# Scores of a key tile issued ahead of its first max multiplication, in a one-core attention layer

## The chip, the cores and the metric

One Trainium2 chip, one of its cores. The time is device microseconds (us) of one execution of the whole program on that core; a kernel's time is the median of several executions.

## What is computed

A self-attention layer with a residual, for 16 batches of 1024 tokens with 512 features and 8 heads of 64. Queries, keys and values are the same projection `q`. The mask is 0 or 1 for each token, with about half of them 1. Cut to what matters:

```python
xt = jnp.transpose(x, (0, 2, 1))
q = xt @ Wq.T
qh = q.reshape(B, T, NH, dk).transpose(0, 2, 1, 3)
scores = scale * jnp.einsum('bhqd,bhkd->bhqk', qh, qh)
logits = (scores * cmask + (1.0 - cmask) * NEG) * rmask      # cmask: keys, rmask: queries
attn = jax.nn.softmax(logits, axis=-1)
ctx = jnp.einsum('bhqk,bhkd->bhqd', attn, qh)
out = ctx.transpose(0, 2, 1, 3).reshape(B, T, D) @ Wo.T
return x + jnp.transpose(out, (0, 2, 1))
```

## The kernel before

Tokens with mask 0 need no attention of their own: their result is one mean vector for each batch. So the kernel gathers the tokens with mask 1 of a batch into 5 tiles of 108 rows (540 columns, the form called "small"), runs attention on these alone, and scatters the results back. For each batch there are 8 heads, and for each head 5 steps, one for each key tile k. All the work of a batch is laid out on these 40 steps (h, k) by tables that are written out by hand, the same for every engine; each engine runs its own list in its own order, and semaphores join them. Batches 2 to 13 run in a loop whose body is two batches.

In step (h, k) TensorE has this to do, in the order of the code:

- `max_scores`, twice: the scores of head h+2, key tile k, one call for each half of the queries (m = 2k and m = 2k+1), one matmul of 270 columns each, line L1041. VectorE reduces each of them to a row maximum (`reduce_max`, L845). They go to two PSUM banks, `MX[0]` for even m and `MX[1]` for odd m, so multiplication m waits until reduction m-2 is done (semaphore `mx_red`). I call them M0 to M9 of a head, and the reductions R0 to R9.
- `scores`: the scores of head h, key tile k, both halves, two passes (L1056 and L1059), four matmuls in all, into three PSUM banks `ST`. ScalarE turns them into exponentials `Pt` (L715). Half 0 of a step waits for the exponential three uses of a bank back, half 1 for the first exponential of the step before. I call them S0 to S4 of a head.
- `misc`: pieces of other work from the table. A projection (`proj`, L1102, twelve matmuls), an output tile (`out`, L1102, twelve of 512 columns) and the mean row (`w`, L1128) come in two parts, part 0 ahead of the odd max multiplication, part 1 at the end of the step. `V` (L1148, L1150) is in part 0 of steps 0 and 1 of odd heads; `xT` (L1114) and `mT` (L1155) are at the end of a step.
- In step 2 of each head: `L`, the sums of the exponentials of the head before (L1160), which waits for GpSimd's last addition of that head (`Pacc`, L557), and then `times_values`, twenty matmuls of that head (L1069).

VectorE's list has the reduction of each max multiplication, and between them the rest: after the even reduction of a step the low part of a projection (L860), the two passes that finish an output tile (L925, L929) or the low part of `xT` (L867), each from the step before; then `scale` (L896), `reciprocal` (L875) and, in step 1 of odd heads behind R2, `ctx_low` (L880), a tensor_tensor with both inputs in SBUF. After R9 of a head comes a small reduction (L850).

A step of TensorE's list in the code (`table[h, k]` holds its misc jobs; the two calls of `misc` are its two parts):

```python
max_scores(s + 2, 2 * b + (h + 2) // SLOTS, h + 2, 2 * k)
scores(s, (HEADS // 2) * b + h // 2, h, k)
misc(table[h, k], b, par, s, 0)
if ahead:
    max_scores(s + 2, 2 * b + (h + 2) // SLOTS, h + 2, 2 * k + 1)
```

Of the kernel before, what the change touches and what calls it, by code (L numbers as in the profile page):

```python
# [29 lines left out]
HEADS = 8  # L30
# [186 lines left out]
def at_least(eng, sem, value):  # L217

    if not isinstance(value, int) or value > 0:
        eng.wait_ge(sem, value)  # L220
# [10 lines left out]
def attention_kernel(nc, x_rows, mask_t, wq, wqT, woT, out_rows, B, T, D):  # L231
# [6 lines left out]
    with ExitStack() as ctx:  # L238
# [747 lines left out]
        def _(pe):  # L986
# [11 lines left out]
            def body(f, t, plan):  # L998
# [27 lines left out]
                def tile_cols(i):  # L1026
                    return slice(R * i, R * i + R)

                def half_cols(i):
                    return slice(H * i, H * i + H)  # L1030
# [13 lines left out]
                def scores(s, s2, h, k):  # L1044

                    ops = t["ops"][:, h % SLOTS]
                    if k == 0:
                        pe.wait_ge(mrow_put[h % 2], 16 * (s2 + 1))
                    banks, count = [], 2 * NT * HEADS
                    for half in range(2):  # L1050
                        u = 2 * (NT * h + k) + half
                        banks.append(ST[u % 3])

                        last_user = u - 3 if u >= 3 else next(v for v in range(-1, -4, -1) if (count + v - u) % 3 == 0)
                        at_least(pe, exp_done, 2 * NT * (s - h) + last_user + 1)
                        nc.tensor.matmul(banks[half][:R, 0:H], ops[:, OPA, tile_cols(k)], ops[:, OPB, half_cols(half)],  # L1056
                                         start=True, stop=False)
                    for half in range(2):
                        nc.tensor.matmul(banks[half][:R, 0:H], ops[:, OPY, tile_cols(k)], ops[:, OPX, half_cols(half)],  # L1059
                                         start=False, stop=True).then_inc(s_ready, 1)  # L1060
# [138 lines left out]
                def batch(b, par, table, has_prev, has_next):  # L1199
                    for h in range(HEADS):  # L1200
                        s = HEADS * b + h
                        for k in range(NT):
                            ahead = h < HEADS - 2 or has_next
                            if ahead:
                                max_scores(s + 2, 2 * b + (h + 2) // SLOTS, h + 2, 2 * k)
                            scores(s, (HEADS // 2) * b + h // 2, h, k)
                            misc(table[h, k], b, par, s, 0)
                            if ahead:
                                max_scores(s + 2, 2 * b + (h + 2) // SLOTS, h + 2, 2 * k + 1)

                            for name, arg, bank, before in table[h, k]:
                                if name == "L" and f.split:
                                    job(name, arg, bank, before, b, par, s - 1)
                            for back, tile in f.values_at.get(k, ()):
                                if h >= back:
                                    times_values(s - back, PAIRS * b + (h - back) // 2, h - back, tile)
                                elif has_prev:
                                    times_values(s - 1, PAIRS * b - 1, HEADS - 1, tile)
                            misc(table[h, k], b, par, s, 1)

                def tail(jobs):
# [4 lines left out]
                    for name, arg, bank, before in jobs:  # L1226
                        job(name, arg, bank, before, B, B % 2, HEADS * B - 1)

                run_batches(pe, f, plan, batch, tail)

            fitting_form(pe, body)
# [25 lines left out]
```

## Time and profile before

| what | value |
|---|---|
| time, median of 3 runs | 1811.57 us (1807.76 to 1812.94) |
| the profiled execution's own time | 1810.9 us |
| its span in the trace | 1809.2 us |
| mean granted TensorE clock | 0.954 of full speed |
| TensorE matmuls busy | 1649.8 us, 91% of the span |
| VectorE busy | 1186.7 us, 66% |
| ScalarE busy | 847.6 us, 47% |
| GpSimd busy | 1355.1 us, 75% |

Busy time is work that the trace shows, and a share of the span. The 1.7 us between the span and the execution's own time lie outside the program's instructions. "PE" is TensorE, "PEld" its weight loads, "DVE" VectorE, "ACT" ScalarE, "POOL" GpSimd. Matmuls overlap, so a matmul of 270 columns lasts 0.29 us in the trace while the next starts 0.12 to 0.13 us after it.

### The profile page before, as it was taken

How to read it: one execution, taken by the hardware profiler on the slowest of the kernel's cores; microseconds unless marked ns; L12 is line 12 of the kernel's file. 1: busy time of each engine (PE TensorE's matmuls, PEld its weight loads, DVE VectorE, ACT ScalarE, POOL GpSimd, SP SyncE). 2: the span in 40 equal slices, each digit the busy share in tenths (PEclk: the TensorE clock that was granted, in tenths of full speed). 3: DMA queues.
4: the chain of work that ended last, by engine and by line, in shares of the span. 5: the costliest groups of instructions: out<-in, count | busy, mean ns of one | idle time of the engine just before them, and what ended most of it. 6: DMA issues, size and time to landing. Idle time of an engine off the chain costs nothing.

```text
span 1809.2 us, 40177 instructions
## 1 busy us (share of the span) xinstructions
PE 1649.8 (91%) x10956; PEld 1259.5 (70%) x10956; DVE 1186.7 (66%) x2704; ACT 847.6 (47%) x2055; POOL 1355.1 (75%) x1165
## 2 busy tenths in 40 slices
PE   6588999999899999989899998999999999999995
PEld 4457777777667777777667776677776677777763
DVE  5347676666757766576766767566675666767663
ACT  1136455454545545364544636445453554546451
POOL 5358787788868877787768878678786877789752
PEclk9679999999999999999999999999999999999998
DMA  3234353444435353353424444353443434344310
GB/s 102 71 83 108 85 129 78 129 93 109 116 83 129 75 138 85 101 122 93 128 61 128 97 103 118 72 137 78 122 103 90 118 80 131 82 116 108 100 48 27
DMA packets 93883, 179.86 MB, mean 99 GB/s; under 512 B 24704, under 2 KB 24832, under 8 KB 93632
## 3 DMA queue, kind: packets, MB, share of 16 engines
q1 hardware_dynamic: 64448, 109.71, 26.5%
q0 software_dynamic: 29184, 67.17, 12.9%
q8 instruction: 113, 1.85, 0.4%
q14 instruction: 138, 1.13, 0.2%
HBM read 36.77 MB, written 33.55 MB: 39 GB/s over the span
## 4 chain that ended last, share of the span: by engine, by line
PE 36%; POOL 30%; issue 23%; DVE 5%; ACT 2%; DMA 2%; POOLq 1%; SPq 0%; DVEq 0%; ACTq 0%
POOL small_Pacc L557 16%; PE misc L1102 10%; PE ctx_psum L1069 8%; POOL small_xg L491 6%; PE max_scores L1041 4%; PE scores L1056 4%; PE scores L1059 3%; POOL out_rows L498 3%; POOL small_xsum L545 3%; PE misc L1160 2%; DVE small_mxp L845 2%; PE misc L1128 2%; DMA out_rows<-small_xg,small_idx_cur 2%; ACT small_Pt L715 1%; POOL small_xg L509 1%
## 5 line engine op out<-in xcount | busy, mean ns | idle before, releaser
L845 DVE TENSOR_REDUCE small_mxp<-max_scores 108x1 f32<-108x270 f32 x1280 | 539.4, 435 | 402.5 <-PE max_scores L1041 369.4
L715 ACT ACTIVATE small_Pt<-scores,small_kbias 108x270 f32<-108x270 f32 x1280 | 551.9, 484 | 447.4 <-PE scores L1059 419.3
L557 POOL TENSOR_TENSOR small_Pacc<-small_Pacc,small_Pt 108x540 f32<-108x540 f32 x384 | 537.7, 1400 | 164.1 <-ACT small_Pt L715 153.9
L1041 PE MATMUL max_scores<-small_ops 128*108 128x270 f32 x1280 | 408.6, 339 | 63.4 <-DVE small_mxp L845 60.5
L1041 PEld LDWEIGHTS max_scores<-small_ops 128*108 128x108 f32 x1280 | 223.6, 178 | 154.2 <-DVE small_mxp L845 87.9
L1069 PE MATMUL ctx_psum<-small_Pt,small_V 108*64 108x270 f32 x2560 | 323.3, 400 | 0.0
L875 DVE RECIPROCAL small_rsum<-small_rsum 128x67 f32<-128x67 f32 (+1 forms) x512 | 241.2, 534 | 120.0 <-ACT small_rsum L661 120.0
L1056 PE MATMUL scores<-small_ops 128*108 128x270 f32 x1280 | 300.7, 306 | 4.8 <-ACT small_Pt L715 3.8
L1069 PEld LDWEIGHTS ctx_psum<-small_Pt,small_V 108*64 108x64 f32 x2560 | 192.3, 141 | 113.0 <-issue 11.8
L1059 PE MATMUL scores<-small_ops 128*108 128x270 f32 x1280 | 269.6, 293 | 0.0
L491 POOL DMA_INDIRECT small_xg<-x_rows,small_idx_cur x160 | 165.4, 1034 | 103.9 <-POOL small_idx_cur L484 65.4
L1056 PEld LDWEIGHTS scores<-small_ops 128*108 128x108 f32 x1280 | 203.5, 177 | 39.8 <-ACT small_Pt L715 24.8
L498 POOL DMA_INDIRECT out_rows<-small_xg,small_idx_cur x160 | 164.7, 1029 | 67.1 <-issue 22.3
L1059 PEld LDWEIGHTS scores<-small_ops 128*108 128x108 f32 x1280 | 196.1, 177 | 0.0
L557 POOL TENSOR_TENSOR small_Pacc<-small_Pt 108x540 f32<-108x540 f32 x128 | 171.7, 1342 | 29.3 <-ACT small_Pt L715 27.7
L646 ACT CAST small_H<-misc 128x270 fp32r<-128x270 f32 x128 | 49.3, 385 | 229.1 <-PE misc L1102 223.8
L545 POOL TENSOR_TENSOR small_xsum<-small_xsum,small_xg 108x512 f32<-108x512 f32 x120 | 153.6, 1280 | 0.4
L1102 PE MATMUL misc<-small_xcT,small_wqT_hi 128*128 128x270 f32 x512 | 151.6, 296 | 1.8 <-DVE small_xcT_lo L867 1.3
L509 POOL TENSOR_TENSOR small_xg<-small_xg,small_w 108x512 f32<-108x512 f32 (+1 forms) x80 | 111.5, 1393 | 55.0 <-ACT small_w L635 44.0
L1102 PE MATMUL misc<-small_xcT_lo,small_wqT_hi 128*128 128x270 f32 x512 | 148.1, 289 | 0.0
L1102 PE MATMUL misc<-small_xcT,small_wqT_lo 128*128 128x270 f32 x512 | 147.9, 289 | 0.0
L1102 PE MATMUL misc<-small_woT_hi,small_ctxT 128*108 128x512 f32 x320 | 132.0, 413 | 6.9 <-DVE small_ctxT_lo L880 6.8
(106 smaller groups left out, 2238.7 us busy)
## 6 DMA issues: line engine op xcount, KB each, us to landing
small_ops<-small_H SPq DMA_DIRECT2D x512, 135.0 KB
small_ops<-small_L SPq DMA_DIRECT2D x256, 135.0 KB
small_xg<-x_rows,small_idx_cur POOLq DMA_INDIRECT x160, 3.5
out_rows<-small_xg,small_idx_cur POOLq DMA_INDIRECT x160, 3.4
small_ops<-small_mrow SPq DMA_DIRECT2D x128, 2.1 KB
wq_sb<-wq SPq DMA_DIRECT2D x1, 1024.0 KB, 5.7
woT_sb<-woT SPq DMA_DIRECT2D x1, 1024.0 KB, 7.8
wqT_sb<-wqT SPq DMA_DIRECT2D x1, 1024.0 KB, 9.8
```

The costliest lines, as they stand in the source:

```text
L491: nc.gpsimd.indirect_dma_start(out=t["xg"][:r, par, k, :], out_offset=None, in_=x_rows, in_offset=bass.IndirectOffsetOnAxis(ap=t["idx_cur" ...
L498: nc.gpsimd.indirect_dma_start(out=out_rows, in_=t["xg"][:r, par, k, :], in_offset=None, out_offset=bass.IndirectOffsetOnAxis(ap=t["idx_cu ...
L545: nc.gpsimd.tensor_tensor(acc[:r], other, t["xg"][:r, par, k, :], ALU.add).then_inc(xsum_step, 1)
L557: nc.gpsimd.tensor_tensor(acc, other, t["Pt"][:R, p0], ALU.add).then_inc(pacc_step, 1)
L715: nc.scalar.activation(t["Pt"][:R, (NT * h + k) % f.NP, half, :], ST[(2 * (NT * h + k) + half) % 3][:R, 0:H], ACT.Exp, bias=t["kbias"][:R, ...
L845: nc.vector.tensor_reduce(t["mxp"][:R, h % 2, m // 2, m % 2:m % 2 + 1], MX[m % 2][:R, 0:H], AX.X, ALU.max).then_inc(mx_red, 1)
L875: nc.vector.reciprocal(t["rsum"][:, cols], t["rsum"][:, cols]).then_inc(recip_step, 1)
L1041: nc.tensor.matmul(MX[m % 2][:R, 0:H], ops[:, OPA, tile_cols(m // 2)], ops[:, OPB, half_cols(m % 2)], start=True, stop=True).then_inc(mx_r ...
L1056: nc.tensor.matmul(banks[half][:R, 0:H], ops[:, OPA, tile_cols(k)], ops[:, OPB, half_cols(half)], start=True, stop=False)
L1059: nc.tensor.matmul(banks[half][:R, 0:H], ops[:, OPY, tile_cols(k)], ops[:, OPX, half_cols(half)], start=False, stop=True).then_inc(s_ready, 1)
L1069: last = nc.tensor.matmul(CT[DK * half:DK * half + DK, 0:H], t["V"][:R, (h // 2) % 2, k, DK * (h % 2):DK * (h % 2) + DK], t["Pt"][:R, (NT ...
L1102: last = nc.tensor.matmul(out, lefts[a][left_at], rights[z][right_at], start=(c == 0 and i == 0), stop=(c == KD - 1 and i == 2))
```

## The change

In each step (h, k) the four score matmuls are issued ahead of the even max multiplication, and no longer behind it. Nothing else is altered: the same instructions with the same waits, and no other engine's list changes.

```diff
                             ahead = h < HEADS - 2 or has_next
+                            scores(s, (HEADS // 2) * b + h // 2, h, k)
                             if ahead:
                                 max_scores(s + 2, 2 * b + (h + 2) // SLOTS, h + 2, 2 * k)
-                            scores(s, (HEADS // 2) * b + h // 2, h, k)
                             misc(table[h, k], b, par, s, 0)
                             if ahead:
                                 max_scores(s + 2, 2 * b + (h + 2) // SLOTS, h + 2, 2 * k + 1)
```

TensorE's list where no misc job stands between the max multiplications: the end of head 5 (M9) and steps 0 to 2 of head 6, up to `L`. Before, each S stands between an even M and the next odd one:

```order
 L1041 MATMUL max_scores<-small_ops 108x270 x2
 L1056 MATMUL scores<-small_ops 108x270 x2
 L1059 MATMUL scores<-small_ops 108x270 x2
 L1041 MATMUL max_scores<-small_ops 108x270 x2
 L1056 MATMUL scores<-small_ops 108x270 x2
 L1059 MATMUL scores<-small_ops 108x270 x2
 L1041 MATMUL max_scores<-small_ops 108x270
 L1155 MATMUL misc<-ident,small_mcol 5x108
 L1041 MATMUL max_scores<-small_ops 108x270
 L1056 MATMUL scores<-small_ops 108x270 x2
 L1059 MATMUL scores<-small_ops 108x270 x2
 L1041 MATMUL max_scores<-small_ops 108x270
```

The same place after the change, from M8 and M9 of the last step of head 5 on (S4 stands ahead of them):

```order
 L1041 MATMUL max_scores<-small_ops 108x270 x2
 L1056 MATMUL scores<-small_ops 108x270 x2
 L1059 MATMUL scores<-small_ops 108x270 x2
 L1041 MATMUL max_scores<-small_ops 108x270 x2
 L1056 MATMUL scores<-small_ops 108x270 x2
 L1059 MATMUL scores<-small_ops 108x270 x2
 L1041 MATMUL max_scores<-small_ops 108x270 x2
 L1155 MATMUL misc<-ident,small_mcol 5x108
 L1056 MATMUL scores<-small_ops 108x270 x2
 L1059 MATMUL scores<-small_ops 108x270 x2
 L1041 MATMUL max_scores<-small_ops 108x270 x2
```

Before, the pairs of M that follow each other are an odd one and the next step's even one; after, they are the two of one step, and M4 and M5 both stand behind S2, right ahead of `L`.

TensorE's list in steps 1 and 2 of head 5, where `V` jobs (L1148, L1150) stand in step 1. Before:

```order
 L1041 MATMUL max_scores<-small_ops 108x270 x2
 L1056 MATMUL scores<-small_ops 108x270 x2
 L1059 MATMUL scores<-small_ops 108x270 x2
 L1148 MATMUL misc<-identR,small_H 108x128
 L1150 MATMUL misc<-identR,small_L 108x128
 L1041 MATMUL max_scores<-small_ops 108x270
 L1155 MATMUL misc<-ident,small_mcol 5x108
 L1041 MATMUL max_scores<-small_ops 108x270
 L1056 MATMUL scores<-small_ops 108x270 x2
 L1059 MATMUL scores<-small_ops 108x270 x2
 L1041 MATMUL max_scores<-small_ops 108x270
 L1160 MATMUL misc<-small_Pacc,ones 64x270 x2
```

After, from M1 on; M2 has moved behind S1, and M4 behind S2:

```order
 L1041 MATMUL max_scores<-small_ops 108x270
 L1056 MATMUL scores<-small_ops 108x270 x2
 L1059 MATMUL scores<-small_ops 108x270 x2
 L1041 MATMUL max_scores<-small_ops 108x270
 L1148 MATMUL misc<-identR,small_H 108x128
 L1150 MATMUL misc<-identR,small_L 108x128
```

The last step of the batch ahead of the loop's jump and the first steps behind it (a jump and its registers are L386 and L220), before:

```order
 L1128 MATMUL misc<-G,small_xbarT 128x512 x2
 L1041 MATMUL max_scores<-small_ops 108x270
 L1056 MATMUL scores<-small_ops 108x270 x2
 L1059 MATMUL scores<-small_ops 108x270 x2
 L1041 MATMUL max_scores<-small_ops 108x270
 L386 UNCONDITIONAL_BRANCH
 L386 ISA
 L220 ISA
 L1041 MATMUL max_scores<-small_ops 108x270
```

And after:

```order
 L1128 MATMUL misc<-G,small_xbarT 128x512 x2
 L1056 MATMUL scores<-small_ops 108x270 x2
 L1059 MATMUL scores<-small_ops 108x270 x2
 L1041 MATMUL max_scores<-small_ops 108x270 x2
 L386 UNCONDITIONAL_BRANCH
 L386 ISA
 L220 ISA
 L1056 MATMUL scores<-small_ops 108x270 x2
 L1059 MATMUL scores<-small_ops 108x270 x2
```

The first work behind the jump is S0 in place of M0.

## Rows read from the trace of the kernel before

**Rows 1.** The page: busy us, share of the span and instructions of each engine.

```profile
PE 1649.8 (91%) x10956; PEld 1259.5 (70%) x10956; DVE 1186.7 (66%) x2704; ACT 847.6 (47%) x2055; POOL 1355.1 (75%) x1165
```

**Rows 2.** Waits: engine, line <- waited for: us in total, times, longest.

```profile
PE max_scores L1041 <- DVE small_mxp L845: 60.5, 77, 4.3
PE misc L1114 <- ACT small_xv L688: 22.1, 44, 1.2
PE misc L1160 <- POOL small_Pacc L557: 12.0, 18, 2.7
```

**Rows 3.** Timeline, TensorE, into head 6: start, us, what, [idle before <-releaser].

```profile
1019.74 0.29 PE L1041 MATMUL max_scores<-small_ops 128*108 128x270 f32 x1
...
1020.37 0.62 PE L1041 MATMUL max_scores<-small_ops 128*108 128x270 f32 x2
...
1022.00 0.38 PE L1041 MATMUL max_scores<-small_ops 128*108 128x270 f32 x1 [0.20 <-DVE small_mxp L845]
...
1023.80 0.29 PE L1041 MATMUL max_scores<-small_ops 128*108 128x270 f32 x1
1024.02 0.68 PE L1160 MATMUL misc<-small_Pacc,ones 108*64 108x270 f32 x4
```

**Rows 4.** Timeline, VectorE, the same stretch.

```profile
1019.66 0.44 DVE L896 TENSOR_TENSOR small_ctx<-small_rsum,ctx_psum 64x270 f32<-64x270 f32 x1
1020.12 0.44 DVE L845 TENSOR_REDUCE small_mxp<-max_scores 108x1 f32<-108x270 f32 x1
...
1020.95 0.43 DVE L845 TENSOR_REDUCE small_mxp<-max_scores 108x1 f32<-108x270 f32 x1
...
1021.51 1.34 DVE L845 TENSOR_REDUCE small_mxp<-max_scores 108x1 f32<-108x270 f32 x3
1023.04 0.89 DVE L845 TENSOR_REDUCE small_mxp<-max_scores 108x1 f32<-108x270 f32 x2 [0.19 <-PE max_scores L1041]
```

**Rows 5.** Timeline, all engines, steps 1 and 2 of head 5, batch 8.

```profile
1011.49 0.45 PE L1041 MATMUL max_scores<-small_ops 128*108 128x270 f32 x2
...
1012.37 2.08 POOL L557 TENSOR_TENSOR small_Pacc<-small_Pacc,small_Pt 108x540 f32<-108x540 f32 x1 [0.17 <-POOL small_Pacc L557]
...
1012.55 0.71 DVE L880 TENSOR_TENSOR small_ctxT_lo<-small_ctx,small_ctxT 128x540 fp32r<-128x540 f32 x1
...
1013.66 0.37 PE L1041 MATMUL max_scores<-small_ops 128*108 128x270 f32 x1
...
1014.51 0.45 PE L1160 MATMUL misc<-small_Pacc,ones 108*64 108x270 f32 x2 [0.47 <-POOL small_Pacc L557]
```

**Rows 6.** Timeline, all engines, the same steps of batch 7.

```profile
901.90 1.91 DVE L880 TENSOR_TENSOR small_ctxT_lo<-small_ctx,small_ctxT 128x540 fp32r<-128x540 f32 x1
901.90 1.32 POOL L557 TENSOR_TENSOR small_Pacc<-small_Pacc,small_Pt 108x540 f32<-108x540 f32 x1
...
904.21 0.37 PE L1041 MATMUL max_scores<-small_ops 128*108 128x270 f32 x1 [1.30 <-DVE small_mxp L845]
```

**Rows 7.** Timelines, TensorE and VectorE, around the loop's jump.

```profile
936.42 0.37 PE L1041 MATMUL max_scores<-small_ops 128*108 128x270 f32 x1 [1.50 <-DVE small_mxp L845]
...
939.41 0.56 PE L1041 MATMUL max_scores<-small_ops 128*108 128x270 f32 x1 [1.89 <-DVE small_mxp L845]
...
938.91 0.79 DVE L845 TENSOR_REDUCE small_mxp<-max_scores 108x1 f32<-108x270 f32 x2 [3.13 <-issue]
```

**Rows 8.** Timelines: TensorE, head 3 of batch 7; VectorE, R8 of head 2, batch 8.

```profile
875.87 0.37 PE L1041 MATMUL max_scores<-small_ops 128*108 128x270 f32 x1 [0.50 <-DVE small_mxp L845]
877.23 0.38 PE L1041 MATMUL max_scores<-small_ops 128*108 128x270 f32 x1 [0.99 <-DVE small_mxp L845]
...
981.71 0.44 DVE L845 TENSOR_REDUCE small_mxp<-max_scores 108x1 f32<-108x270 f32 x1 [1.34 <-PE max_scores L1041]
```

**Rows 9.** Windows: us, busy of PE, PEld, DVE, ACT, POOL, PEclk, DMA share, GB/s.

```profile
938.00:945.00 7.00, 5.59 (x27) 4.19 (x29) 3.14 (x8) 3.12 (x8) 4.64 (x4) 0.53 0.30 70
982.00:998.50 16.50, 13.62 (x85) 10.39 (x84) 11.90 (x29) 10.41 (x24) 11.89 (x13) 0.79 0.46 126
```

## The prediction

> **What bounds the kernel now.** I read the page first: TensorE's matmuls fill 91% of the span and no other engine passes 75% [rows 1]. TensorE's list sets the time, and only its waits and lost clock can move, since the change adds and removes no instruction. The view of waits says which they are. TensorE waits 60.5 us in front of max multiplications for VectorE's reductions, 22.1 us in `xT` for ScalarE and 12.0 us in `L` for GpSimd [rows 2]. The 60.5 us are what the change can touch. In the timeline of TensorE, cut by head and step, they lie in three places: behind the jump of the loop, five times in the program, 3.4 us in the one shown [rows 7]; at M1 and M2 of head 3 in each batch, 1.5 us in batch 7 [rows 8]; and at M5 of head 5, 1.3 us where `ctx_low` was slow [rows 6]. Small ones (0.20 us at M2) stand in head 6 [rows 3]. All other waits belong to engines whose lists stay as they are.
>
> **What moves.** A group S is four matmuls. Between M8 and M9 of head 5 stands one such group, and they start at 1019.74 and 1020.37 [rows 3]: 0.63 us, of which M8 itself is 0.13, so S is 0.50 us. After the change each even M is issued 0.50 us later with respect to the work behind it, each odd M at the same time, and S 0.13 us earlier. Total TensorE work is the same. From this follows a rule for any stretch in which VectorE's reductions are the slower side:
> - It starts with VectorE idle until some M arrives. If that M is even, the stretch starts 0.50 us later; if it is odd, at the same time.
> - It ends with TensorE waiting at some M. If that M is even, the S that used to stand behind it has already run in the wait, which gives 0.50 us back; if it is odd, S was done in both orders and nothing comes back.
>
> So even start and odd end is a loss of up to 0.50 us, odd start and even end a gain of as much, the others nothing. I go through the places with it.
>
> *Head 3, 15 batches.* The stretch starts at M8 of head 2 (even) and ends at M2 of head 3 (even), where TensorE waits 0.99 us in batch 7 after 0.50 us at M1 [rows 8]. Start +0.50, end -0.50: I take 0.05 us each for one more weight load that nothing covers, 0.8 us in all. Bounds: -0.5 to +0.5 us each, if only one end counts.
>
> *Head 6, 15 batches.* Between `ctx` ending at 1020.10 and R8 at 1020.12 VectorE has no gap, and R8 also starts only 0.38 us after its M8 [rows 3, 4]. With M8 at 1020.24, R8 starts at 1020.62 and not at 1020.12. Behind it: R9 (before, 1020.95 to 1021.38) ends at 1021.88, R0 at 1022.45, R1 at 1022.79. TensorE has done S4, M8, M9 and S0 by 1021.1 and stands at M1 until 1021.94; then S1 takes it to 1022.65, M2 goes at once, M3 at 1022.85, S2 to about 1023.6, M4 at 1023.6. R2 must wait for M2 (1022.65 + 0.36), ends at 1023.45, and R3 at 1023.88. M5 goes at 1023.94, where it went at 1023.80 [rows 3]. Of the 0.50 us there were 0.2 us of idle time on VectorE before R3 [rows 4] and about 0.15 us in TensorE's own waits to swallow, so +0.15 us remain, on the path since `L` follows M5 at once. 15 times 0.15 is 2.2 us. Head 0 of the batches that start without a jump looks alike but has more room at M5: nothing. Heads 1, 5 and 7 have a `V` job between M0 and M1, in which VectorE runs idle now and so catches up; I take 0.02 us for each of these 48 (a max multiplication that now stands uncovered), 1.0 us. Heads 1, 2 and 4 have output tiles or projections ahead of M5, so it never waits there: nothing.
>
> *Head 5, steps 1 and 2.* Here VectorE runs `ctx_low` behind R2. M1 and M2 were issued together from 1011.49 on [rows 5]; now S1 is between them, M2 goes at about 1012.15, R2 ends at 1012.94 in place of 1012.63, and `ctx_low` starts at 1012.85 in place of 1012.55. GpSimd's addition, the one for which `L` waits, started at 1012.37 and was stretched to 2.08 us while `ctx_low` ran in its 0.71 us; in batch 7, where `ctx_low` came while GpSimd was at the end of one operation and at the start of the next, it was VectorE that lost: 1.91 us, and M5 waited 1.30 us [rows 5, 6]. 9 of the 15 batches are of the first kind, 6 of the second or nearly so. Being 0.3 us later, `ctx_low` now meets an addition that is 0.5 us old. If GpSimd wins, its addition takes 1.34 us and ends at 1013.71, `ctx_low` ends at 1014.35, R3 at 1014.80, M5 goes at 1014.86 and `L` at 1015.0, against 1014.51 [rows 5]: +0.48 us in each of 9, 4.3 us. If VectorE still wins, M5 goes at 1013.98, inside the 0.47 us that `L` waits for GpSimd anyway: nothing. Both were seen when the addition was 0.2 to 0.3 us old, so I take half, 2.2 us. The second kind is unchanged: both requests fall into the same addition.
>
> The Trainium skill, "SBUF — State Buffer", section "Who interferes with whom", says that a VectorE instruction with two SBUF inputs contends with a GpSimd one that reads SBUF, and that the first to issue keeps the shared port for the whole instruction. By that rule the later `ctx_low` always loses and the term is the full 4.3 us. The trace agrees in part: the two do stretch each other, but in batch 8 the addition has the earlier start in the records and is the one that was stretched [rows 5].
>
> *The loop's jump, 5 times.* VectorE does nothing for 3.13 us for no reason but its own issue, and R0 starts at 938.91; TensorE has a gap of its own of 1.50 us at its first instruction, then waits at M2 until 939.41 [rows 7]. With S0 and S1 ahead of M2, S1 runs in that wait and need not run after it; the clock is at half there (0.53 granted [rows 9]), so S1 is worth 0.9 us, 0.5 at full clock. But R8 ahead of the jump depends on M8, which is now 0.5 us later, so R0 and M2 come 0.5 us later. Net -0.4 us at half clock, 0 at full clock, +0.2 if M3 then waits too: I take -0.2 us, -1.0 us in all. Bounds -0.9 to +0.5 us each.
>
> *`xT` in heads 3 and 4.* The 0.5 us waits there (22.1 us [rows 2]) are ScalarE's own chain of copy, multiplication and two exponentials, which is busy without a gap, and the exponential already finds its scores. Nothing.
>
> **Sum.** 0.8 + 2.2 + 1.0 + 2.2 - 1.0 = +5.2 us with the terms as taken. They are single values of things that round to nothing, so I shade the two smallest-grained (0.8 and 1.0) to half and forecast +4.3 us: 1810.9 + 4.3 = 1815.2 us for the profiled execution. Its 1810.9 lies 0.7 us below the median, 1811.57. The median should so be 1815.9; I write 1815.5.
>
> **Rivals.**
> 1. *No delay reaches the end, within 0.3%* in either direction: this is my forecast too, as 0.3% is 5.4 us, about what a measurement of this kernel can tell from no change.
> 2. *VectorE is starved at every light head.* If the 0.50 us at even M's were paid in full before each `L` whose M5 has under 0.35 us of slack (head 6, head 0 of 9 batches, and heads 5 and 7: 54 places), 0.35 us each would give 19 us: 1830 us. Against it: the V jobs of heads 5 and 7 hide it, by the rows of head 5. With GpSimd winning at head 5 everywhere (+4.3) and head 6 at 0.3 us (+4.5), with the losses of head 3 at 0.2 (+3), and no gain at the jump, it is +12 us: 1823 us. It decides from 0.36 us a batch on.
> 3. *Faster.* The one mechanism: TensorE now has S to do while it waits at even M's. If VectorE's start of these stretches does not follow M8, because it was late with its own work anyway, the gain stands alone: head 3 gives 0.5 us in 15 batches, 7.5, and the jump 0.9 in five, 4.5: -12 us, 1799.5 us. For it: VectorE's passes over the output tile are what delays R9 in head 3. Against it: they follow R8 in its list, and R8 had 1.34 us of idle time ahead of it [rows 8], so it does follow M8.
> 4. *The clock.* It falls to half behind the waits of head 3 and of the jump; over the 16.5 us of head 3 in batch 8, 0.79 was granted [rows 9], so 16.5 x 0.21 x 2 = 6.9 us at half speed, of which TensorE would lose 3.5 us if it had work all the time; part of it is spent in waits, and I count 2 us. Where TensorE's idle time is split otherwise, falls can come or go in each of 15 batches; if a third of them changed, 10 us, of either sign. It widens the range and is in the chances of both sides.
>
> **How the numbers follow.** Within 0.3% (forecast and rival 1): 0.46. Slower than that (rival 2, or the clock on that side): 0.37. Faster (rival 3, or the clock): 0.17. The likeliest case alone is 1806 to 1817 us; the range reaches to rival 2's milder form and half of rival 3: 1804 to 1826 us.
>
> **What would show it.** In the profile after: the wait at M2 behind the jump shorter by 0.5 us or more than the 1.89 us of [rows 7], with R0 about 0.5 us later after the last M9; in head 3 a wait at M1 that has grown by 0.5 us and at M2 shrunk by as much; in head 6 a wait at M1 of 0.6 to 0.9 us that is not there now, and M5 to M5 of light heads longer by 0.15 us; `ctx_low` in head 5 at 1.3 to 1.9 us in more batches than 6, with GpSimd's addition back at 1.34 us. Wrong if the time between two `L` of heads 6 and 7 grows by 0.4 us or more, if head 3 gets shorter, or if head 5 does not change while the total moves by over 5 us.

## The result and the profile after

The changed kernel takes 1867.38 us, median of 4 runs (1866.02 to 1869.61), against 1810.14 us (1807.76 to 1812.94, 4 runs) for the kernel before: a ratio of 1.0317, 95% interval 1.0296 to 1.0337. The forecast was 1815.5 us, at most 1826. The profiled execution spans 1867.9 us at a mean granted clock of 0.945, 58.7 us more than before. By the rows of busy times TensorE was busy for 16.3 us more, on the same matmuls, and idle for 42.4 us more.

The page's row of busy times after, which answers to [rows 1]:

```profile
PE 1666.1 (89%) x10956; PEld 1268.6 (68%) x10956; DVE 1244.7 (67%) x2704; ACT 847.2 (45%) x2055; POOL 1333.8 (71%) x1165
```

Not one instruction was added, yet VectorE is busy for 58.0 us more and GpSimd for 21.3 us less. An engine whose busy time grows on an unchanged list has instructions that last longer. The view of instruction groups names them. Columns: line, operation, out<-in, shapes, count | busy us, mean ns | idle before. First the two groups of VectorE that differ, before:

```profile
L929 DVE SCALAR_TENSOR_TENSOR small_xg<-small_w,small_inv,small_xsum 108x512 f32<-108x512 f32 x80 | 60.3, 753 | 2.8
L880 DVE TENSOR_TENSOR small_ctxT_lo<-small_ctx,small_ctxT 128x540 fp32r<-128x540 f32 x64 | 56.7, 886 | 2.8 <-ACT small_ctxT L680 2.8
```

And after:

```profile
L929 DVE SCALAR_TENSOR_TENSOR small_xg<-small_w,small_inv,small_xsum 108x512 f32<-108x512 f32 x80 | 115.6, 1444 | 2.8
L880 DVE TENSOR_TENSOR small_ctxT_lo<-small_ctx,small_ctxT 128x540 fp32r<-128x540 f32 x64 | 64.2, 1003 | 2.8 <-ACT small_ctxT L680 2.8
```

L929 is the second of the two passes that finish an output tile; both its large inputs, `w` and `xsum`, lie in SBUF. The prediction names it only as part of "VectorE's passes over the output tile". It grew by 55.3 us and `ctx_low` (L880) by 7.5; the other groups of VectorE kept their length to within 2 us in all. (The page's busy time counts overlapping instructions once and so grew less than the two together.) TensorE's waits that changed; first, before, those that [rows 2] does not have:

```profile
PE misc L1102 <- DVE small_ctxT_lo L880: 6.8, 3, 4.9
PE scores L1056 <- ACT small_Pt L715: 3.8, 12, 0.5
PE misc L1160 <- DVE small_xcT_lo L867: 3.3, 7, 0.5
```

And after:

```profile
PE max_scores L1041 <- DVE small_mxp L845: 74.0, 72, 4.2
PE scores L1056 <- ACT small_Pt L715: 25.6, 72, 1.6
PE misc L1114 <- ACT small_xv L688: 17.9, 46, 1.2
PE misc L1102 <- DVE small_ctxT_lo L880: 13.5, 16, 4.9
PE misc L1160 <- DVE small_xcT_lo L867: 11.8, 13, 1.0
PE misc L1160 <- POOL small_Pacc L557: 7.1, 6, 2.7
```

The largest growth in this view, 21.8 us, is that of S for ScalarE's exponentials. It lies at S0 of heads 0, 1 and 6 (0.32, 0.22 and 0.20 us in most batches, 1.2 to 1.6 in head 0 behind the jump) and at S1 of head 0 behind the jump. The stretches into heads 0 and 6 hardly grew by it, as the table below shows; in head 1 it counts.

To find where the time went, I took the time from `L` in head h to `L` in the next head, mean over batches 1 to 13, in us:

| stretch | 1 to 2 | 2 to 3 | 3 to 4 | 4 to 5 | 5 to 6 | 6 to 7 | 7 to 0 | 0 to 1 | sum |
|---|---|---|---|---|---|---|---|---|---|
| before | 17.06 | 17.90 | 11.94 | 11.92 | 9.64 | 10.79 | 14.81 | 11.95 | 106.0 |
| after | 17.09 | 20.63 | 12.78 | 11.96 | 9.70 | 10.75 | 14.83 | 12.54 | 110.3 |
| change | +0.03 | +2.73 | +0.84 | +0.04 | +0.06 | -0.04 | +0.02 | +0.59 | +4.3 |

The 4.3 us a batch are 55 us in these 13 batches, nearly all of the 58.7. They lie in three stretches.

**Head 2 to head 3, +2.73 us.** The end of head 2 in batch 8, timelines of VectorE and then of GpSimd, before (R8's row is in [rows 8]):

```profile
982.18 0.75 DVE L925 SCALAR_TENSOR_TENSOR small_xsum<-misc,small_valid,small_xg 108x512 f32<-108x512 f32 x1
982.97 0.75 DVE L929 SCALAR_TENSOR_TENSOR small_xg<-small_w,small_inv,small_xsum 108x512 f32<-108x512 f32 x1
983.64 0.43 DVE L860 TENSOR_TENSOR small_L<-misc,small_H 128x270 fp32r<-128x270 f32 x1
983.99 0.43 DVE L845 TENSOR_REDUCE small_mxp<-max_scores 108x1 f32<-108x270 f32 x1
...
979.97 1.00 POOL L498 DMA_INDIRECT out_rows<-small_xg,small_idx_cur  x1 [0.19 <-issue]
...
982.10 1.02 POOL L491 DMA_INDIRECT small_xg<-x_rows,small_idx_cur  x1 [0.93 <-POOL small_idx_cur L484]
983.15 1.76 POOL L557 TENSOR_TENSOR small_Pacc<-small_Pacc,small_Pt 108x540 f32<-108x540 f32 x1
```

The same place after, VectorE, GpSimd and TensorE's M1 of head 3:

```profile
1012.18 1.86 DVE L929 SCALAR_TENSOR_TENSOR small_xg<-small_w,small_inv,small_xsum 108x512 f32<-108x512 f32 x1
...
1016.13 0.44 DVE L845 TENSOR_REDUCE small_mxp<-max_scores 108x1 f32<-108x270 f32 x1 [0.71 <-PE max_scores L1041]
1016.61 0.75 DVE L925 SCALAR_TENSOR_TENSOR small_xsum<-misc,small_valid,small_xg 108x512 f32<-108x512 f32 x1
1017.39 2.63 DVE L929 SCALAR_TENSOR_TENSOR small_xg<-small_w,small_inv,small_xsum 108x512 f32<-108x512 f32 x1
1019.95 0.43 DVE L860 TENSOR_TENSOR small_L<-misc,small_H 128x270 fp32r<-128x270 f32 x1
1020.29 0.42 DVE L845 TENSOR_REDUCE small_mxp<-max_scores 108x1 f32<-108x270 f32 x1
...
1012.12 1.36 POOL L557 TENSOR_TENSOR small_Pacc<-small_Pacc,small_Pt 108x540 f32<-108x540 f32 x1
1014.94 1.00 POOL L498 DMA_INDIRECT out_rows<-small_xg,small_idx_cur  x1 [1.46 <-DVE small_xg L929]
...
1017.08 1.03 POOL L491 DMA_INDIRECT small_xg<-x_rows,small_idx_cur  x1 [0.93 <-POOL small_idx_cur L484]
1018.14 1.33 POOL L557 TENSOR_TENSOR small_Pacc<-small_Pacc,small_Pt 108x540 f32<-108x540 f32 x1
...
1020.77 0.38 PE L1041 MATMUL max_scores<-small_ops 128*108 128x270 f32 x1 [2.38 <-DVE small_mxp L845]
```

Before, L929 took its 0.75 us and GpSimd's addition beside it was the one stretched, from 1.34 to 1.76. After, the addition has its 1.33 us and L929 lasts 2.63, and 1.86 one step earlier. Both end 0.55 us after the addition beside them (1020.02 against 1019.47, 1014.04 against 1013.48). The second case is not one of a VectorE that comes later: L929 starts 0.75 us ahead of the addition where it was 0.18 ahead before. It is GpSimd that has moved, since its scatter L498 had waited 1.46 us for the stretched L929 of the step before (before, it sat idle for 0.19 us and not for L929), and everything behind it came later. One stretch so set up the next. R9 stands behind L929 in VectorE's list, and M1 of head 3 waits for R9: 2.38 us where [rows 8] has 0.50. So it is in every batch: over batches 1 to 13 the waits at M1 of head 3 have a mean of 2.38 us (before 0.49), those at M2 of 0.45 (before 1.18). TensorE's idle time in this stretch, all of its gaps added up, went from 2.01 to 4.07 us. Of the 2.06 us more, 1.15 are the waits for reductions, 0.54 are `L`'s wait for the low part of `xT` (L867), 0.23 are the first `V` job's wait (put down to the first pass, L925), and the rest is small. The wait for L867 is not L929's doing: it is 0.99 us in the experiment below in which all steps but three have the new order and L929 is back at 0.75.

**Head 3 to head 4, +0.84 us.** This is the clock. Windows of one stretch each, columns as in [rows 9]; before, heads 3 to 4 of batch 7, and heads 2 to 3 of batch 8:

```profile
880.68:892.32 11.64, 10.20 (x77) 7.76 (x77) 8.75 (x21) 8.53 (x20) 8.00 (x10) 1.00 0.56 150
972.01:990.56 18.55, 16.64 (x100) 13.32 (x100) 12.02 (x27) 7.52 (x18) 14.56 (x15) 0.87 0.44 121
```

After, heads 2 to 3 and 3 to 4 of batch 7:

```profile
891.02:911.60 20.58, 16.62 (x101) 12.85 (x100) 15.08 (x28) 8.15 (x19) 14.28 (x16) 0.88 0.39 101
911.60:925.80 14.20, 13.12 (x78) 8.89 (x78) 8.60 (x21) 8.20 (x19) 9.01 (x9) 0.82 0.49 122
```

By the clock's record in the trace, TensorE had half speed (1.2 of 2.4 GHz) in heads 3 to 4 for 0.59 us a batch before and 2.22 after; half of the 1.63 more is 0.82 us, the whole difference. Two kernels below have the new order and no fall of the clock here, and need 11.72 and 11.76 us. In heads 2 to 3 it was 2.56 before and 4.35 after, so up to 0.9 of the 2.73 us there is clock too; 0.67 are left when the idle time is taken off.

**Head 0 to head 1, +0.59 us.** In head 1 of batch 8, `ctx_low` beside GpSimd's last multiplication of an output tile (L509), and the first matmul of the output tile in step 2, before:

```profile
952.02 2.11 POOL L509 TENSOR_TENSOR small_xg<-small_xg,small_w 52x512 f32<-52x512 f32 x1
...
952.28 0.71 DVE L880 TENSOR_TENSOR small_ctxT_lo<-small_ctx,small_ctxT 128x540 fp32r<-128x540 f32 x1
...
953.26 0.48 PE L1102 MATMUL misc<-small_woT_hi,small_ctxT 128*108 128x512 f32 x1
```

And after:

```profile
985.12 1.28 POOL L509 TENSOR_TENSOR small_xg<-small_xg,small_w 52x512 f32<-52x512 f32 x1
...
985.94 1.04 DVE L880 TENSOR_TENSOR small_ctxT_lo<-small_ctx,small_ctxT 128x540 fp32r<-128x540 f32 x1
...
987.13 0.45 PE L1102 MATMUL misc<-small_woT_hi,small_ctxT 128*108 128x512 f32 x1 [0.46 <-DVE small_ctxT_lo L880]
```

`ctx_low` starts 0.82 us after L509 in place of 0.26, is stretched, and the output tile, which needs it, waits 0.46 us where it waited for nothing. Over batches 1 to 13 the waits for `ctx_low` here grew from 0.14 to 0.54 us a batch. The other 0.21 us is S0 of head 1, which now waits for ScalarE.

### The profile page after: what moved, and what is told of

It reads as the page before. It is cut to its first block, busy times and chain, and to the rows that moved or that the text cites. A ratio compares the mean times of both kernels' runs of the same rounds, so it can differ in the third digit from the quotient of the medians.

```text
span 1867.9 us, 40177 instructions
## 1 busy us (share of the span) xinstructions
PE 1666.1 (89%) x10956; PEld 1268.6 (68%) x10956; DVE 1244.7 (67%) x2704; ACT 847.2 (45%) x2055; POOL 1333.8 (71%) x1165
## 3 DMA queue, kind: packets, MB, share of 16 engines
q14 instruction: 138, 1.13, 0.2%
## 4 chain that ended last, share of the span: by engine, by line
PE 68%; issue 9%; POOL 9%; DVE 8%; ACT 4%; SPq 0%; POOLq 0%; ACTq 0%; DVEq 0%; DMA 0%
PE misc L1102 21%; PE ctx_psum L1069 14%; PE scores L1056 8%; PE max_scores L1041 7%; PE scores L1059 6%; PE misc L1160 4%; PE misc L1128 3%; POOL small_Pacc L557 3%; POOL small_xg L491 3%; ACT small_Pt L715 3%; DVE small_mxp L845 2%; DVE small_ctxT_lo L880 2%; DVE small_xg L929 1%; PE misc L1114 1%; PE misc L1150 1%
## 5 line engine op out<-in xcount | busy, mean ns | idle before, releaser
L557 POOL TENSOR_TENSOR small_Pacc<-small_Pacc,small_Pt 108x540 f32<-108x540 f32 x384 | 516.4, 1345 | 199.7 <-ACT small_Pt L715 192.0
L1041 PE MATMUL max_scores<-small_ops 128*108 128x270 f32 x1280 | 363.3, 319 | 74.8 <-DVE small_mxp L845 74.0
L1056 PE MATMUL scores<-small_ops 128*108 128x270 f32 x1280 | 338.9, 328 | 30.4 <-ACT small_Pt L715 25.6
L1069 PE MATMUL ctx_psum<-small_Pt,small_V 108*64 108x270 f32 x2560 | 331.9, 408 | 0.0
L1059 PE MATMUL scores<-small_ops 128*108 128x270 f32 x1280 | 270.3, 293 | 0.0
L498 POOL DMA_INDIRECT out_rows<-small_xg,small_idx_cur x160 | 163.6, 1022 | 120.9 <-DVE small_xg L929 81.4
L491 POOL DMA_INDIRECT small_xg<-x_rows,small_idx_cur x160 | 168.8, 1055 | 103.9 <-POOL small_idx_cur L484 52.5
L545 POOL TENSOR_TENSOR small_xsum<-small_xsum,small_xg 108x512 f32<-108x512 f32 x120 | 160.6, 1338 | 0.4
L509 POOL TENSOR_TENSOR small_xg<-small_xg,small_w 108x512 f32<-108x512 f32 (+1 forms) x80 | 102.4, 1280 | 54.7 <-ACT small_w L635 43.9
```

Source lines behind the costliest of these rows:

```text
L491: nc.gpsimd.indirect_dma_start(out=t["xg"][:r, par, k, :], out_offset=None, in_=x_rows, in_offset=bass.IndirectOffsetOnAxis(ap=t["idx_cur" ...
L498: nc.gpsimd.indirect_dma_start(out=out_rows, in_=t["xg"][:r, par, k, :], in_offset=None, out_offset=bass.IndirectOffsetOnAxis(ap=t["idx_cu ...
L545: nc.gpsimd.tensor_tensor(acc[:r], other, t["xg"][:r, par, k, :], ALU.add).then_inc(xsum_step, 1)
L557: nc.gpsimd.tensor_tensor(acc, other, t["Pt"][:R, p0], ALU.add).then_inc(pacc_step, 1)
L1041: nc.tensor.matmul(MX[m % 2][:R, 0:H], ops[:, OPA, tile_cols(m // 2)], ops[:, OPB, half_cols(m % 2)], start=True, stop=True).then_inc(mx_r ...
L1069: last = nc.tensor.matmul(CT[DK * half:DK * half + DK, 0:H], t["V"][:R, (h // 2) % 2, k, DK * (h % 2):DK * (h % 2) + DK], t["Pt"][:R, (NT ...
```

## The experiments

The theory: the change delays VectorE behind the even M's by 0.5 us, by which L929 and `ctx_low` come at other places against GpSimd's instructions and lose to them, and their longer time reaches TensorE. The rival: the delay itself, or the new order of TensorE's list, costs the time, and the stretched L929 is off the path. Ratios are against executions of the kernel before that were measured alongside; times between `L`'s are as in the table.

**L929 reads PSUM in place of SBUF.** The first pass writes its result back to the PSUM bank, and the bank is held until the second pass is done. Once in the new order, once in the old.

```diff
-  scalar_tensor_tensor(out=t["xsum"][:R], in0=MB[bank][:R, 0:D],
+  scalar_tensor_tensor(out=MB[bank][:R, 0:D], in0=MB[bank][:R, 0:D],
...
-  in1=t["xsum"][:R], op0=ALU.mult, op1=ALU.add).then_inc(out_done, 1)
+  in1=MB[bank][:R, 0:D], op0=ALU.mult, op1=ALU.add).then_inc(out_done, 1)
...
-  at_least(pe, out_step, NT * (b - 1) + arg + 1)
+  at_least(pe, out_done, NT * (b - 1) + arg + 1)
```

> The changed order, but the first finishing pass of an output tile leaves its result in its PSUM bank and the second pass (L929) reads it from there, so that the second pass has one input from SBUF and not two; TensorE may reuse the bank only when the second pass is done. Theory 1 (VectorE's second finishing pass is caught behind GpSimd's additions): L929 is 0.75 us in all 80 places, and the time falls from 1867 to 1810 to 1820 us. Rival, theory 2 (VectorE is starved in all steps because each even max multiplication comes 0.5 us later): the time stays above 1855 us. Rival, theory 3 (TensorE's clock falls more often): it stays above 1850 us unless the falls go too.

> The same edit of the finishing passes on the kernel before. L929 is 0.75 us there already, so theory 1 expects no change, 1806 to 1814 us; the later release of the bank costs nothing, since the next user of a bank comes two jobs later. Theory 2 and 3 say the same. If it is slower by 5 us or more, the edit itself has a price that must be taken off e1.

New order: 1834.14 us, 1.0132 (1.0097 to 1.0168). Old order: 1806.39 us, 0.9987 (0.9969 to 1.0005). The group of L929 and TensorE's waits with the new order:

```profile
L929 DVE SCALAR_TENSOR_TENSOR small_xg<-small_w,small_inv,misc 108x512 f32<-108x512 f32 x80 | 59.8, 747 | 2.8
```

```profile
PE max_scores L1041 <- DVE small_mxp L845: 37.3, 57, 2.0
...
PE misc L1148 <- DVE small_xg L929: 15.2, 15, 1.0
...
PE misc L1102 <- DVE small_xg L929: 8.9, 15, 0.6
```

The first of the two waits for L929 with the old order, where the second is not there:

```profile
PE misc L1148 <- DVE small_xg L929: 7.7, 15, 0.5
```

L929 is back at 0.75 us, the waits for reductions are half of what they were, and 33 of the 57 us are gone. The kernel did not get down to the 1820 us that I allowed: the held bank brought two waits, 15.2 and 8.9 us, of which the old order pays 7.7 and nothing. That it is its SBUF reads that L929 loses over is shown; that all the rest is the edit's price is not. Nor is the gain one of waits alone: against the changed kernel TensorE's idle time fell by only 10.3 us, its busy time by 25.6, and the time at half clock from 209.1 to 130.8 us (table at the end of this section).

**Which steps carry the loss.** The new order in all steps but three, and in those three alone: (1,3), (2,3) and (2,4), the ones whose even reduction stands ahead of an L929 that was stretched.

```diff
+ first = (h, k) not in ((1, 3), (2, 3), (2, 4))     # the other kernel: in
+ if first:
+     scores(s, (HEADS // 2) * b + h // 2, h, k)
  if ahead:
      max_scores(s + 2, 2 * b + (h + 2) // SLOTS, h + 2, 2 * k)
+ if not first:
+     scores(s, (HEADS // 2) * b + h // 2, h, k)
```

> The new order in all steps but (1,3), (2,3) and (2,4), which keep the old one; the slow second passes (tiles 0, 3 and 4) stand behind the even reductions of these three. Theory 1: the three passes come at nearly their old time against GpSimd's additions, L929 goes back to 0.75 us in most places, 1810 to 1822 us. Theory 2: three of 40 steps, so the loss shrinks by some 8%, to 1862 us.

> The old order in all steps but (1,3), (2,3) and (2,4), which have the new one. Theory 1: most of the loss is here, 1845 to 1870 us, with L929 at 1.5 to 2.6 us for tiles 0, 3 and 4. Theory 2: 8% of the loss, 1815 us.

All but three: 1820.36 us, 1.0060 (1.0033 to 1.0087), L929 at 0.76 us, heads 2 to 3 at 17.27 us. The three alone: 1840.98 us, 1.0167 (1.0129 to 1.0206), a little less than the 1845 that I expected at least, heads 2 to 3 at 20.27 us, and L929:

```profile
L929 DVE SCALAR_TENSOR_TENSOR small_xg<-small_w,small_inv,small_xsum 108x512 f32<-108x512 f32 x80 | 110.0, 1375 | 2.8
```

Three steps of 40 carry over half of the loss. The two parts add up to 2.3% and not 3.2. TensorE's idle time does add up: 22.9 and 19.2 us more than before, against 42.4 with both. Its busy time does not: 15.1 us less and 14.1 more, against 16.3 more. That points to the clock, which was at half speed for 46.3 us less and 18.5 more, against 38.8 more; half of each is what it can cost. So the 0.6% of the other 37 steps hides 22.9 us of idle time behind a gain of the clock. (The stretches themselves don't add up either: with both, L929 is longer in the last two steps of head 2, 1.87 and 2.63 us against 1.46 and 2.23, and shorter in head 1, 1.47 against 1.9.)

**The delay without the new order.** The kernel before, with one more VectorE reduction of 0.43 us per output tile, whose result nothing uses: between the two passes, so that L929 starts later, or behind L929, so that only what follows is later.

```diff
+  nc.vector.tensor_reduce(t["spare"][:R, k:k + 1], t["w"][:R, par, 0:H], AX.X, ALU.max)
```

> The kernel before, its order untouched, with one extra VectorE reduction of 270 columns (0.43 us, its result is not used) between the two finishing passes of each output tile, so that the second pass L929 starts some 0.4 us later. Theory 1 (what counts is where L929 starts against GpSimd's additions): L929 goes from 0.75 us to 1.4 to 2.6 us for tiles 0, 3 and 4, and the time rises to 1835 to 1865 us, though TensorE's order is the old one. Rival (only VectorE's amount of work or TensorE's order counts): as e6, L929 stays at 0.75 us.

> The same extra reduction behind the second finishing pass: the same VectorE work, but L929 starts where it did. Theory 1: L929 stays at 0.75 us, and the time is 1808 to 1822 us, the 0.43 us of five tiles in 16 batches (34 us of VectorE time) lying mostly in its idle time. If e5 and e6 are equal, theory 1 falls.

Ahead of L929: 1823.64 us, 1.0084 (1.0062 to 1.0107). Behind it: 1807.24 us, 1.0002 (0.9984 to 1.0021). The group of L929, first ahead:

```profile
L931 DVE SCALAR_TENSOR_TENSOR small_xg<-small_w,small_inv,small_xsum 108x512 f32<-108x512 f32 x80 | 101.7, 1271 | 0.0
```

Then behind:

```profile
L930 DVE SCALAR_TENSOR_TENSOR small_xg<-small_w,small_inv,small_xsum 108x512 f32<-108x512 f32 x80 | 60.3, 753 | 2.8
```

This parts the theories best. The same 0.43 us of delay to R9 costs nothing behind L929 and 15 us ahead of it: not the delay costs, but what it does to L929. The size was a little over half of the 28 us that I expected at least. The timelines of VectorE and GpSimd show a part of the reason, in batch 8 and, last two rows, in batch 9, at the end of head 2:

```profile
996.60 2.67 DVE L931 SCALAR_TENSOR_TENSOR small_xg<-small_w,small_inv,small_xsum 108x512 f32<-108x512 f32 x1
...
996.33 1.02 POOL L492 DMA_INDIRECT small_xg<-x_rows,small_idx_cur  x1 [0.93 <-POOL small_idx_cur L485]
997.38 1.32 POOL L558 TENSOR_TENSOR small_Pacc<-small_Pacc,small_Pt 108x540 f32<-108x540 f32 x1
...
1101.94 0.74 DVE L931 SCALAR_TENSOR_TENSOR small_xg<-small_w,small_inv,small_xsum 108x512 f32<-108x512 f32 x1
...
1101.68 1.02 POOL L492 DMA_INDIRECT small_xg<-x_rows,small_idx_cur  x1 [0.92 <-POOL small_idx_cur L485]
```

With the same starts to 0.01 us, it is stretched in the one and not in the other; of the 16 at this place 9 stayed at 0.74 (the last of them is at its normal length in every kernel). The offset of the starts makes a loss likely, it does not decide it.

**VectorE's list changed in place of TensorE's.** The late jobs of a step (the two passes, the low parts) stand ahead of the even reduction and not behind it, so that L929 starts before GpSimd's addition whatever M does. Everywhere with the new order, everywhere with the old, and with the old in steps (2,3) and (2,4) only.

```diff
  for a in range(2):
+     early = a == 0 and (h, k) in ((2, 3), (2, 4))     # everywhere: a == 0
+     if early:
+         for name, arg, bank, before in due:
+             job(name, arg, bank, b, par, s - 1)
      if h < HEADS - 2 or has_next:
          reduce_max(s + 2, h + 2, 2 * k + a)
...     # where not early, the same jobs stand here, as before
```

> The changed order on TensorE, and on VectorE the work of the step before (finishing passes, low parts of projections and of xT) ahead of the even reduction of a step and not behind it. The even max multiplication comes 0.5 us later after the change, and VectorE stands idle for it; now the passes use that time. Theory 1: L929 comes some 0.9 us earlier than after the change, ahead of GpSimd's addition again for tiles 3 and 4, and 1805 to 1825 us; below 1800 us if the reductions are not the path. Theory 2 (reductions starved): the even reductions come later still, 1870 us or more.

> The same VectorE order on the kernel before. There the even max multiplication is issued at once, so the passes delay its reduction by 0.4 to 1.5 us: theory 1 expects L929 some 0.4 us earlier, out of reach of most additions or behind the end of the one before, 1805 to 1825 us; theory 2 expects a loss of 0.4 us or more in each step with such work, 1820 to 1840 us.

> The kernel before with one edit on VectorE: in steps (2,3) and (2,4) alone the work of the step before (the finishing passes of tiles 3 and 4, and a projection's low part) goes ahead of the even reduction. In e8, which did it everywhere, the stretch from L of head 2 to L of head 3 became 1.6 us shorter than before and the other heads 0.4 to 1.1 us longer. Theory 1: the passes start 0.45 us earlier and M1 of head 3 is released earlier: 1.2 to 1.8 us in 15 batches, 1780 to 1792 us. If e8's losses and gains don't separate by head, 1800 to 1815 us.

| kernel | us | ratio (95%) | L929, mean us | heads 2 to 3, us |
|---|---|---|---|---|
| new order, everywhere | 1818.10 | 1.0057 (1.0039 to 1.0075) | 0.754 | 15.70 |
| old order, everywhere | 1835.16 | 1.0161 (1.0144 to 1.0178) | 0.759 | 16.29 |
| old order, two steps | 1791.41 | 0.9915 (0.9888 to 0.9942) | 0.756 | 16.72 |

With the new order the loss of 3.2% falls to 0.6% without a word changed in TensorE's list. Not all of that is the stretch undone: heads 2 to 3 get shorter with the old order as well (17.90 to 16.29 us), where L929 was never stretched. With the old order everywhere the time came out where the rival had it, 1820 to 1840 us. Everywhere, the edit also delays even reductions that TensorE waits for: with the old order heads 1 to 2 go from 17.06 to 18.11 us and heads 5 to 6 from 9.64 to 10.35. In the two steps alone it has no such price and beats both kernels, by 0.85% the one before. Its windows of heads 2 to 3 and 3 to 4 in batch 8 say where its gain lies:

```profile
965.49:982.19 16.70, 14.69 (x100) 11.54 (x100) 11.99 (x28) 7.84 (x19) 12.64 (x14) 1.00 0.45 120
982.19:993.84 11.65, 10.21 (x78) 7.77 (x78) 8.75 (x21) 8.54 (x20) 8.77 (x10) 1.00 0.57 144
```

The clock does not fall there in any of batches 1 to 13. Before, it was at half for 2.56 + 0.59 us a batch in the two, which can cost 1.6 us at most; the two are 1.43 us shorter. The waits for reductions in head 3 are 0.43 us shorter (1.24 us a batch against 1.67), but `L` waits 0.26 us longer for L867 and another job 0.20 longer for ScalarE, so that TensorE's idle time in the two stretches is the same, 3.5 us a batch in both kernels. The gain is the clock's.

**Both in the same two steps,** and **the `ctx_low` steps.** The last kernel with TensorE's new order in its two steps as well; then the new order in all steps but (1,1), (1,3), (2,3), (2,4) and (5,1); then in (1,1) and (5,1) alone, the steps of `ctx_low`.

```diff
+ first = (h, k) in ((2, 3), (2, 4))     # with early as above
+ first = (h, k) not in ((1, 1), (1, 3), (2, 3), (2, 4), (5, 1))
+ first = (h, k) in ((1, 1), (5, 1))
```

> As e9, and in the same two steps TensorE's new order (scores ahead of the even max multiplication). In e7 the stretch from L of head 2 to L of head 3 was 2.2 us shorter than before. Theory 1: 2.0 to 2.4 us in 15 batches less, 1772 to 1785 us; then the changed order is good just where its damage was, once the passes don't stand behind the later reduction. Theory 2 (late even reductions cost whatever stands around them): no better than e9, or slower.

> The new order in all steps but (1,3), (2,3), (2,4), as in e3, and also not in (1,1) and (5,1), whose even reductions stand ahead of ctx_low. e3 left 11.5 us over before. Theory 1 (the rest of the loss is ctx_low behind GpSimd's operation, and the output tile in (1,2) that waits for it): 3 to 7 us over before go away, 1808 to 1814 us. Theory 2: the other 35 steps still have the new order, so no more than 5 of 37 of e3's loss, 1818 us.

> The old order but in (1,1) and (5,1), the steps with ctx_low that lost after the change. Theory 1: 4 to 10 us slower than before, by 0.5 us at the output tile of (1,2) and 0 to 0.5 us in head 5. Theory 2: within 1 us of before (0.5 us in two even multiplications of 80).

Both: 1791.62 us, 0.9909 (0.9877 to 0.9941), not to be told from VectorE's edit alone; TensorE's order adds nothing even there, as the rival had it. (1791.62 is the median of six executions, one of which took 3323 us for an unknown reason; of the other five it is 1790.53, and the ratio is theirs.) All but five: 1813.41 us, 1.0035 (1.0018 to 1.0053). The two `ctx_low` steps alone: 1820.63 us, 1.0076 (1.0052 to 1.0099), 12 us, more than I had expected. In it heads 0 to 1 are 0.77 us longer and heads 3 to 4 0.46, and in the second the clock was at half for 1.52 us a batch and not 0.59, half of which difference is 0.46. But with the old order in (1,1) and the new one around it, heads 0 to 1 are at 12.47 us as well: `ctx_low` of head 1 lasts 1.3 to 1.5 us in most batches there too. Either shift, in its own step or in those ahead of it, is enough to make it lose. What it costs differs: there TensorE waits 0.29 us a batch for it (0.54 after the change, 0.14 before) and 0.21 for ScalarE at S0, a wait that the kernel with the two steps alone does not have. Head 5 has next to no part: heads 4 to 5 are at 11.89 us.

**Idle time and clock apart.** TensorE in the profiled executions, us; its matmuls are the same in all, and idle is span less busy. Half of a difference in the last column is the most that the clock can have made. Busy time moves by other things too, since a matmul's recorded length is not fixed at one clock: with the new order in the three steps it grew by 14.1 us, and the clock explains 9.3 of that at most.

| kernel | idle | busy | clock at half |
|---|---|---|---|
| before | 159.4 | 1649.8 | 170.3 |
| after | 201.8 | 1666.1 | 209.1 |
| new order, L929 reads PSUM | 191.5 | 1640.5 | 130.8 |
| new order but in three steps | 182.3 | 1634.7 | 124.0 |
| new order in the three | 178.6 | 1663.9 | 188.8 |
| old order, delay ahead of L929 | 169.6 | 1657.8 | 168.8 |
| old order, delay behind L929 | 154.2 | 1647.8 | 154.1 |
| old order, VectorE's list, everywhere | 214.3 | 1617.7 | 99.6 |
| old order, VectorE's list, two steps | 164.1 | 1627.9 | 113.6 |

The clock goes with the kernel and not with the execution: granted on average were 0.943 to 0.945 in all four of the kernel after, 0.948 to 0.961 in those of the kernel before, 0.964 to 0.969 in all six of the last. More idle time does not mean less clock: the last but one idles most and was at half speed least. What makes the clock fall was not tried by itself.

## Why the prediction was wrong

**The step that failed** is the one on head 3: "Start +0.50, end -0.50: I take 0.05 us each for one more weight load that nothing covers". The start did shift, and the wait at M2 did shrink (1.18 to 0.45 us). But the rule on starts and ends holds only if what VectorE does in between keeps its length. It was applied as if it did, to a stretch that contains two instructions whose length depends on when they start. Measured there: +2.73 us a batch, and +0.84 behind it by the clock, 50 us over batches 0 to 14 in place of 0.8. The wait at M1 of head 3 grew by 1.89 us where 0.5 was forecast, that at M2 shrank by 0.73.

The evidence was in the trace before: GpSimd's addition took 1.76 us beside L929 and 1.34 elsewhere. The prediction read exactly this from `ctx_low` and addition in head 5 [rows 5, 6], and priced it there only. The rival 3 named the passes over the output tile as what delays R9, and looked only at whether they start late.

**Heads 1, 2 and 4, "so it never waits there: nothing".** Wrong for head 1: the output tile itself reads `ctx_low`. +0.59 us a batch, 0.40 of it this wait; 8 us in all.

**S as work that can always run.** The working lets S run as soon as it is issued. S0 of heads 0, 1 and 6 now comes before ScalarE has read the scores of earlier steps: 25.6 us of waits in all, 3.8 before. Only the 0.21 us in head 1 can be seen in the time.

**Head 5.** The mechanism was right: `ctx_low` goes from 0.71 us in 9 of 15 batches to 1.4 to 1.5 in 11 and 1.1 to 2.1 in the other four, its addition back to 1.34, and M5 waits 1.13 us a batch in place of 0.54. But `L` then waits no more for GpSimd (12.0 us in all before, 7.1 after), and heads 4 to 5 grow by 0.04 us, not 0.15.

**Head 6.** Predicted +0.15, measured +0.06 us; the wait at M1 is there with 0.16 us, not 0.6 to 0.9, and the 0.19 us that TensorE waited at M2 is gone in return.

**The jump.** The wait at M2 of head 0 fell from 0.98 to 0.47 us a batch, as said, and that at M0 from 0.44 to nothing, but a wait of 1.2 to 1.6 us behind the jump now stands ahead of S0; heads 7 to 0 are unchanged (+0.02).

**The clock** was a rival of either sign, 10 us. It went the slow way: half speed for 209.1 us in all and not 170.3. Half of the difference, 19 us, is the most that it took, a third of the loss; the 16.3 us by which TensorE's busy time grew fit it. The rival allowed 10. It was not the chance that the rival had it to be, since each kernel keeps its own clock in all of its executions. It fell more where the waits of head 3 had grown. But the sum of these waits does not settle it: with L929 reading PSUM in the old order they are 1.10 us a batch and the clock was at half for 2.63 us in heads 2 to 4, with VectorE's list changed in two steps they are 1.24 us and it never was. Its cause stays open.

Of the forms in which the kernel could get slower, I had only the starved light heads and the clock. The slower side was right in that an even M later makes VectorE late; the price was not in the 0.5 us but in what they met.

## What to carry to other kernels

Before an engine's work is shifted by some tenths of a microsecond, list every instruction on VectorE and GpSimd that the trace shows at two lengths, and every partner that runs beside it: a sum that keeps durations fixed is worth nothing across these. Where the trace has one of them stretched without harm (here GpSimd, off the path), its partner on the path is one small shift from being the victim. A cure that worked here is to fix the order of the two by the list that holds the sensitive one; done in every step it cost elsewhere, so the steps have to be chosen. And part TensorE's idle time from its busy time before a gain or loss is put down to waits: here the clock was up to a third of the loss and, by these sums, the whole of the one gain.

## What the runs showed of the hardware

The 0.50 us by which the even M's moved turned L929 from 0.75 to 1.47, 1.87 or 2.63 us by its place in the batch (against the addition beside it its start moved by 0.2 to 0.9 us), and to 0.75 again where its third operand came from PSUM. The two engines' operations do not share: one keeps its normal time, the other ends a fixed time behind it, 0.55 us for L929 and 0.58 for `ctx_low` (986.98 against 986.40). Where GpSimd lost, in the kernel before, its addition ended 1.2 us behind L929 (984.91 against 983.72), most of its 1.34 us. The Trainium skill, "SBUF — State Buffer", section "Who interferes with whom", says that a VectorE instruction with two SBUF inputs contends with a GpSimd one that reads SBUF, and calls the contention an exclusive lock. The runs agree, and show it for scalar_tensor_tensor.

The Trainium skill also says there that the order of issue decides who blocks. The records' starts do not tell who that is: L929 lost with a start 0.06 us behind the addition and, in the 2.63 us case, 0.75 us ahead of it, while `ctx_low` won with one 0.26 us behind L509. With starts ahead of the addition L929 won at 0.45 us (new order but in three steps) and lost at 0.34 (new order in the three). In the 2.63 us case GpSimd was issuing an indirect DMA (L491) when L929 started, but the same overlap to 0.01 us left L929 at 0.74 us in another batch. What decides it there stays open.
